# Layer-1 keys of a two-layer transformer: where tile 0's values and features stand in the order of work

## The chip, the cores and the metric

One core of a Trainium2 chip runs the whole network in one launch. Its engines work side by side, each through its own list of instructions in a fixed order: TensorE (PE) multiplies matrices, VectorE (DVE), ScalarE (ACT) and GpSimd (POOL) work on elements, SyncE (SP) issues transfers. They meet only at semaphores. The metric is the device time in microseconds; lower is better.

## The reference

The network has two layers of attention and experts over 2048 tokens of width 512, with a layer norm after each of the four blocks. The change is in the third block, layer 1's linear attention. Cut to what matters:

```python
x = _layernorm(x + _L0_ffn_ref(...))      # experts of layer 0: x + shared + routed
# _L1_attn_ref, 16 heads of width 32, 64 features
Q, K, V = heads(x @ qw + qb), heads(x @ kw + kb), heads(x @ vw + vb)
feature_map = lambda t: jax.nn.elu(t @ fw1 + fb1) @ fw2 + fb2
Qm, Km = feature_map(Q), feature_map(K)
KV = jnp.einsum('bhsf,bhsd->bhfd', Km, V)
Z = Km.sum(axis=2)
num = jnp.einsum('bhsf,bhfd->bhsd', Qm, KV)
den = jnp.einsum('bhsf,bhf->bhs', Qm, Z)[..., None]
out = (num / jnp.maximum(den, 1e-06)).transpose(0, 2, 1, 3).reshape(b, s, D) @ ow + ob
```

KV and Z are sums over all tokens, so every token's keys, values and features come first (the stage of keys), and the queries use them afterwards (the stage of queries).

## The kernel before

The tokens lie in 16 tiles of 128. Every fp32 product is made of three passes over two halves of each number (`_hi` and `_lo`, `mm3`, lines 66 to 68). The stage of keys is `attention1_keys`; all engines start it together after the experts of layer 0, and all start the queries together after it. In it the steps are, with i a tile and n a half of a pair of tiles (pair c holds tiles 2c and 2c+1; its halves are n = 2c and 2c+1):

- combine(i), "adding" in the title: GpSimd issues the gathers of the tile's two expert results (L1344; combine(i) issues those of tile i+1, once the buffer is free), VectorE adds them onto the residual (L1572, L1574) and takes the statistics of the layer norm (L93, L95).
- rstd(c), on GpSimd: one over the standard deviation of the pair's tiles (L100, L102).
- normalise(c), on VectorE: the pair's two tiles are normalised (L106).
- turn(n): TensorE transposes one half of the pair's columns into bank 0 (L1406), ScalarE copies out the high part (L1470), VectorE the low part (L1539). Bank 0 is one buffer, so turn(n) waits for the low part of turn(n-1).
- keys(n): 24 matmuls of 256 columns into bank 2 (k_kw), read by ScalarE (L1480) and VectorE (L1548).
- tile(i): 12 matmuls of 512 columns for the values (k_vw) and 16 of 256 for the features (a_fw, L1456) on TensorE. VectorE adds the bias to the values (L1560), ScalarE splits them (L1486) and applies Exp and Relu to the features (L1492, L1493), VectorE takes the low part and joins the two (L1563, L1567), and GpSimd adds the values to a running sum (L1383).
- before_tile(i) and after_tile(i), the end of a tile: ScalarE and GpSimd split the features (L1500, L1389), then TensorE adds the tile's products into KV: 16 small matmuls, L1430 and L1432, called sums(i) below.

The order is written out by hand in `schedule`, and each engine walks through the same list and does its own part of each step; an engine without a part in a step skips it. Up to pair 2 the list is written line by line, then a loop over the tiles runs 6 tiles ahead with combine, 4 halves ahead with turn, 2 ahead with keys. No planner changes this.

Of the kernel before, what the change touches and what calls it, by code (L numbers as in the profile page):

```python
# [31 lines left out]
NT = T // P  # L32
# [1202 lines left out]
def attention1_keys(k, xt, w):  # L1235
# [5 lines left out]
    with ExitStack() as ctx:  # L1241
# [42 lines left out]
        def schedule(turn=idle, keys=idle, tile=idle, before_tile=idle, after_tile=idle, combine=idle, rstd=idle, normalise=idle):  # L1284

            combine(0)
            combine(1)
            rstd(0)  # L1290
            normalise(0)
            combine(2)
            turn(0)
            turn(1)
            combine(3)
            rstd(1)
            keys(0)
            normalise(1)
            keys(1)
            turn(2)  # L1300
            turn(3)
            combine(4)
            combine(5)
            rstd(2)
            normalise(2)
            for i in range(NT):
                if i + 6 < NT:
                    combine(i + 6)
                    if i % 2:
                        rstd((i + 5) // 2)  # L1310
                if i + 4 < NT:
                    turn(i + 4)
                if i + 2 < NT:
                    keys(i + 2)
                if i % 2 and i + 6 < NT:
                    normalise((i + 5) // 2)
                if i:
                    before_tile(i - 1)
                tile(i)
                if i:  # L1320
                    after_tile(i - 1)
            before_tile(NT - 1)
            after_tile(NT - 1)

        with nc.Block() as block:
# [15 lines left out]
            def _(pool):  # L1341
# [43 lines left out]
                def tile_end(i):  # L1385
                    for n in (2 * i, 2 * i + 1):
# [3 lines left out]
                                           ALU.subtract).then_inc(s_glo, 1)  # L1390

                schedule(tile=tile, before_tile=tile_end, combine=combine, rstd=rstd)

            @block.tensor
            def _(pe):
# [40 lines left out]
                def tile(i):  # L1436
# [12 lines left out]
                    for n in (2 * i, 2 * i + 1):  # L1449
# [7 lines left out]
                        mm.then_inc(s_g, 1)  # L1457

                schedule(turn, keys, tile, after_tile=sums)

            @block.scalar
            def _(act):
# [32 lines left out]
                def tile_end(i):  # L1495
                    if i >= 2:
                        act.wait_ge(s_kv, i - 1)
                    for n in (2 * i, 2 * i + 1):
                        act.wait_ge(s_gf, n + 1)
                        act.activation(g_hi[:, i % 2, (n % 2) * CH:(n % 2 + 1) * CH], gf[:, n % 2, :], ACT.Copy).then_inc(s_ghi, 1)  # L1500

                schedule(turn, keys, tile, before_tile=tile_end)

            @block.vector
# [1204 lines left out]
```

## Time and profile before

| | us |
|---|---|
| median of 3 runs | 1599.05 |
| lowest and highest | 1598.6, 1601.68 |
| the profiled execution itself | 1595.75 |

The page's first part, busy time of each engine over the span (share, instructions), and two lines of its second, where each digit is the busy share or the TensorE clock in one fortieth of the span (some 40 us):

```profile
PE 1354.6 (85%) x7253; PEld 1117.2 (70%) x7253; DVE 1075.5 (67%) x1794; ACT 728.8 (46%) x1157; POOL 735.1 (46%) x654
...
PE   5999869999699999936999689996788899999960
...
PEclk8899979999799999968999789997798799999985
```

The stage of keys lies from 688 to 903 us of the span. A low digit of PE is a place where TensorE waits; the fraction of a microsecond is seen only in the timeline of each engine, where a row gives a start, a length, the instruction, and the idle time before it with the work that ended it.

### The profile page before, as it was taken

The numbers are of one execution on the slowest core, as the hardware profiler recorded it, in microseconds if no ns is written. First come the engines' busy times: TensorE is split into PE (matmuls) and PEld (weight loads), VectorE is DVE, ScalarE is ACT, GpSimd is POOL, SyncE is SP. The second block draws the span as 40 slices with busy tenths as digits, with TensorE's granted clock in tenths as the row PEclk, the third lists the DMA queues.
The fourth block names the chain that finished last, engine by engine and source line by source line (L and its number), as shares of the span: only waits on it lengthen the run. The fifth ranks groups of instructions, "written<-read, shape, count | busy, mean of one in ns | idle before, by whom it ended". The sixth has DMA issues, their size and how long they took to land. (4 is left out here: it accounts for less than half of the span.)

```text
span 1594.0 us, 21478 instructions
## 1 busy us (share of the span) xinstructions
PE 1354.6 (85%) x7253; PEld 1117.2 (70%) x7253; DVE 1075.5 (67%) x1794; ACT 728.8 (46%) x1157; POOL 735.1 (46%) x654
## 2 busy tenths in 40 slices
PE   5999869999699999936999689996788899999960
PEld 5787647766377777726999688985566777777740
DVE  5688757232388888865885556674493688888857
ACT  4121132000188888822555354440422488888850
POOL 1445510000488887634664233431055466666634
PEclk8899979999799999968999789997798799999985
DMA  4000040000456566642110000000513899999958
GB/s 166 1 1 27 27 133 2 1 0 0 173 189 215 174 214 220 226 119 55 53 41 1 34 1 1 27 27 27 195 40 115 317 340 344 346 348 344 344 132 316
DMA packets 81807, 212.67 MB, mean 133 GB/s; under 512 B 20425, under 2 KB 23497, under 8 KB 79291
## 3 DMA queue, kind: packets, MB, share of 16 engines
q1 hardware_dynamic: 50075, 133.14, 22.8%
q0 software_dynamic: 31120, 77.38, 17.2%
q8 instruction: 51, 0.84, 0.2%
q10 hardware_dynamic: 528, 1.05, 0.2%
q14 instruction: 33, 0.27, 0.1%
HBM read 208.75 MB, written 46.79 MB: 160 GB/s over the span
## 5 line engine op out<-in xcount | busy, mean ns | idle before, releaser
L66 PE MATMUL bank<-e_w_hi,e_xt_hi 128*96 128x384 f32 (+1 forms) x444 | 168.8, 380 | 3.4 <-DVE e_w_lo L2563 3.4
L2453 POOL DMA_INDIRECT sums<-e_y,r_target_of x64 | 121.8, 1902 | 88.4 <-DMA sums<-e_y,r_target_of 69.7
L68 PE MATMUL bank<-e_w_hi,e_xt_lo 128*96 128x384 f32 (+1 forms) x444 | 161.3, 363 | 0.0
L67 PE MATMUL bank<-e_w_lo,e_xt_hi 128*96 128x384 f32 (+1 forms) x444 | 160.8, 362 | 0.0
L1064 POOL DMA_INDIRECT e_w_raw<-in_w_gate_up,r_load_of x47 | 53.6, 1141 | 215.4 <-issue 215.4
L1189 DVE TENSOR_TENSOR e_w_lo<-e_w_raw,e_w_hi 128x2048 fp32r<-128x2048 f32 x47 | 107.8, 2293 | 33.7 <-ACT e_w_hi L1148 33.7
L2563 DVE TENSOR_TENSOR e_w_lo<-r_w_early,e_w_hi 128x1536 fp32r<-128x1536 f32 x48 | 84.4, 1758 | 24.3 <-ACT e_w_hi L2527 24.3
L1056 POOL DMA_INDIRECT e_xg<-rows,r_token_of x47 | 93.1, 1980 | 14.3 <-issue 14.3
L231 POOL TENSOR_TENSOR a_read<-a_read_n 128x256 f32<-128x256 f32 x64 | 50.3, 785 | 103.0 <-DVE a_read_n L452 103.0
L1687 POOL TENSOR_TENSOR q_g_lo<-q_gf,a_g 128x512 fp32r<-128x512 f32 x32 | 41.6, 1299 | 112.9 <-ACT a_g L1801 112.9
L1148 ACT ACTIVATE e_w_hi<-e_w_raw 128x2048 fp32r<-128x2048 f32 x47 | 89.7, 1909 | 0.0
L66 PE MATMUL bank<-e_w_hi,e_ht_hi 128*96 128x512 f32 (+1 forms) x222 | 87.6, 395 | 2.4 <-DVE e_ht_lo L2575 1.2
L67 PE MATMUL bank<-e_w_lo,e_ht_hi 128*96 128x512 f32 (+1 forms) x222 | 87.3, 393 | 0.0
L68 PE MATMUL bank<-e_w_hi,e_ht_lo 128*96 128x512 f32 (+1 forms) x222 | 87.1, 392 | 0.0
L66 PEld LDWEIGHTS bank<-e_w_hi,e_xt_hi 128*96 128x96 f32 (+1 forms) x444 | 77.4, 174 | 12.3 <-DVE e_w_lo L2563 3.6
L68 PEld LDWEIGHTS bank<-e_w_hi,e_xt_lo 128*96 128x96 f32 (+1 forms) x444 | 77.4, 174 | 11.7
L67 PEld LDWEIGHTS bank<-e_w_lo,e_xt_hi 128*96 128x96 f32 (+1 forms) x444 | 77.8, 175 | 8.6
L66 PE MATMUL bank<-s_xt_hi,s_w_hi 128*128 128x512 f32 (+1 forms) x192 | 76.9, 401 | 0.8 <-ACT s_scores L2212 0.8
L68 PE MATMUL bank<-s_xt_hi,s_w_lo 128*128 128x512 f32 (+1 forms) x192 | 76.1, 396 | 0.0
L67 PE MATMUL bank<-s_xt_lo,s_w_hi 128*128 128x512 f32 (+1 forms) x192 | 75.6, 394 | 0.0
L2527 ACT ACTIVATE e_w_hi<-r_w_early 128x1536 fp32r<-128x1536 f32 x48 | 71.2, 1484 | 0.0
L1072 POOL DMA_INDIRECT e_w_raw<-in_w_down,r_load_of x47 | 60.6, 1290 | 16.4 <-issue 16.4
(461 smaller groups left out, 4335.0 us busy)
## 6 DMA issues: line engine op xcount, KB each, us to landing
r_w_early<-in_w_gate_up SPq DMA_DIRECT2D x48, 768.0 KB, 16.0
r_w_early<-in_w_down SPq DMA_DIRECT2D x24, 768.0 KB, 12.9
results<-e_y SPq DMA_DIRECT2D x47, 256.0 KB, 3.7
rows<-resid SPq DMA_DIRECT2D x8, 1024.0 KB, 4.3
r_w_first<-in_w_gate_up SPq DMA_DIRECT2D x8, 768.0 KB, 15.9
e_w_raw<-in_w_down SPq DMA_DIRECT2D x8, 768.0 KB, 13.2
e_w_raw<-in_w_gate_up SPq DMA_DIRECT2D x8, 768.0 KB, 15.5
resid<-in_x SPq DMA_DIRECT2D x4, 1024.0 KB, 11.5
```

What stands on the lines that cost most here:

```text
L66: pe.matmul(out, a_hi, b_hi, start=start, stop=False)
L67: pe.matmul(out, a_hi, b_lo, start=False, stop=False)
L68: return pe.matmul(out, a_lo, b_hi, start=False, stop=stop)
L231: pool.tensor_tensor(read_2[:, v % 2, :], read_n[:, v % 2, 0:256], read_n[:, v % 2, 256:512], ALU.add).then_inc(s_r2, 1)
L1056: pool.indirect_dma_start(xg[p][:, :], None, k.rows, bass.IndirectOffsetOnAxis(k.token_of[:, c:c + 1], 0)).then_inc(s_g[p], 16)
L1064: pool.indirect_dma_start(w1_raw[p][:, :], None, io["w_gate_up0"], bass.IndirectOffsetOnAxis(k.load_of[:, c:c + 1], 0), bounds_check=E0 * ...
L1072: pool.indirect_dma_start(w2_raw[p][:, :], None, io["w_down0"], bass.IndirectOffsetOnAxis(k.load_of[:, c:c + 1], 0), bounds_check=E0 * P - ...
L1148: act.activation(w1_hi[p][:, :], w1_raw[p][:, :], ACT.Copy).then_inc(s_whi, 1)
L1189: vec.tensor_tensor(w1_lo[p][:, :], w1_raw[p][:, :], w1_hi[p][:, :], ALU.subtract).then_inc(s_wlo, 1)
L2453: pool.indirect_dma_start(k.sums[p % 2], bass.IndirectOffsetOnAxis(k.target_of[:, e:e + 1], 0), y[p][:, :], None, compute_op=ALU.add).then ...
L2527: act.activation(w1_hi[p][:, :, :], w1_raw[p][:, :, :], ACT.Copy).then_inc(s_whi, 1)
L2563: vec.tensor_tensor(w1_lo[p][:, :, :], w1_raw[p][:, :, :], w1_hi[p][:, :, :], ALU.subtract).then_inc(s_wlo, 1)
```

## The change

Tile 0's values and features come right behind turn(3) and combine(4), ahead of combine(5); keys(2) comes ahead of normalise(2) and of turn(4); combine(6) and turn(4) are written out, and the loop starts at tile 1 with the same steps as before. The same instructions run on each engine; only the order is another.

```diff
             turn(2)
             turn(3)
             combine(4)
+            tile(0)
             combine(5)
             rstd(2)
+            keys(2)
             normalise(2)
-            for i in range(NT):
+            combine(6)
+            turn(4)
+            for i in range(1, NT):
                 if i + 6 < NT:
                     combine(i + 6)
                     if i % 2:
...
-                if i:
-                    before_tile(i - 1)
+                before_tile(i - 1)
                 tile(i)
-                if i:
-                    after_tile(i - 1)
+                after_tile(i - 1)
```

On VectorE, from the end of combine(4) on, the order before reads as follows (resid is the residual, k_yg a gathered result, mv mean and variance, a_xt_lo the low part of a turn, k_k_lo that of the keys, k_vf the values):

```order
L1572 SCALAR_TENSOR_TENSOR resid<-k_yg,r_weight,resid 128x512
L1574 SCALAR_TENSOR_TENSOR resid<-k_yg,r_weight,resid 128x512
L93 BN_STATS stats<-resid 128x6
L95 BN_AGGR mv<-stats 128x2
L106 TENSOR_SCALAR resid<-resid,mv,rstd 128x512 x2
L1572 SCALAR_TENSOR_TENSOR resid<-k_yg,r_weight,resid 128x512
L1574 SCALAR_TENSOR_TENSOR resid<-k_yg,r_weight,resid 128x512
L93 BN_STATS stats<-resid 128x6
L95 BN_AGGR mv<-stats 128x2
L1539 TENSOR_TENSOR a_xt_lo<-bank,a_xt_hi 128x2x256
L1548 SCALAR_TENSOR_TENSOR k_k_lo<-bank,k_kb,k_k_hi 128x256 x2
L1560 TENSOR_TENSOR k_vf<-bank,k_vb 128x16x32
```

and in the changed kernel, whose lines stand two further down:

```order
L1562 TENSOR_TENSOR k_vf<-bank,k_vb 128x16x32
L1565 TENSOR_TENSOR k_v_hl<-k_vf,k_v_hl 128x8x66
L1569 SCALAR_TENSOR_TENSOR k_gf<-k_ex,k_gf 128x512 x2
L1574 SCALAR_TENSOR_TENSOR resid<-k_yg,r_weight,resid 128x512
L1576 SCALAR_TENSOR_TENSOR resid<-k_yg,r_weight,resid 128x512
L93 BN_STATS stats<-resid 128x6
L95 BN_AGGR mv<-stats 128x2
L1550 SCALAR_TENSOR_TENSOR k_k_lo<-bank,k_kb,k_k_hi 128x256 x2
L106 TENSOR_SCALAR resid<-resid,mv,rstd 128x512 x2
L1574 SCALAR_TENSOR_TENSOR resid<-k_yg,r_weight,resid 128x512
L1576 SCALAR_TENSOR_TENSOR resid<-k_yg,r_weight,resid 128x512
L93 BN_STATS stats<-resid 128x6
```

The three steps of tile 0 (k_vf, k_v_hl, k_gf) moved ahead of combine(5), and the low part of keys(2) ahead of normalise(2); the low part of turn(4) stays behind combine(6), and after it both orders are the same. TensorE's order changes alike: before turns 2, 3, 4, keys(2), tile(0), turn(5); now turns 2, 3, tile(0), keys(2), turns 4, 5.

On GpSimd, behind the zeroing in combine(4), before (a_vsum is the running sum of the values, a_g the features' low part):

```order
L1344 DMA k_yg<-results,r_slot 128x512 x2
L100 TENSOR_SCALAR var<-mv 128x2
L102 TENSOR_TENSOR rstd<-var,neg_half 128x2
L1344 DMA k_yg<-results,r_slot 128x512 x2
L1383 TENSOR_TENSOR a_vsum<-a_vsum,k_vf 128x528
L1344 DMA k_yg<-results,r_slot 128x512 x2
L100 TENSOR_SCALAR var<-mv 128x2
L102 TENSOR_TENSOR rstd<-var,neg_half 128x2
L1389 TENSOR_TENSOR a_g<-k_gf,a_g 128x512 x2
```

and now:

```order
L1385 TENSOR_TENSOR a_vsum<-a_vsum,k_vf 128x528
L1346 DMA k_yg<-results,r_slot 128x512 x2
L100 TENSOR_SCALAR var<-mv 128x2
L102 TENSOR_TENSOR rstd<-var,neg_half 128x2
L1346 DMA k_yg<-results,r_slot 128x512 x4
L100 TENSOR_SCALAR var<-mv 128x2
L102 TENSOR_TENSOR rstd<-var,neg_half 128x2
L1391 TENSOR_TENSOR a_g<-k_gf,a_g 128x512 x2
```

The sum of tile 0's values moved from behind the gathers of tile 7 to ahead of those of tile 6; the gathers of tiles 7 and 8 now follow each other behind the rstd of pair 2.

## Rows read from the trace of the kernel before

**Rows 1.** The page: the span of the profiled execution.

```profile
span 1594.0 us, 21478 instructions
```

**Rows 2.** Windows of the stage: us, busy (x) of each engine, clock, DMA.

```profile
792.00:802.00 10.00, 10.00 (x77) 9.48 (x76) 8.54 (x12) 4.91 (x10) 6.44 (x7) 1.00 0.16 48
```

**Rows 3.** Waits from 688 to 905 us: total, times, longest us.

```profile
PE bank L1406 <- DVE resid L106: 30.0, 2, 21.7
...
PE bank L1430 <- POOL a_g L1389: 5.0, 2, 3.1
```

**Rows 4.** TensorE timeline: start, length, instruction, [idle before <-releaser].

```profile
728.73 0.66 PE L1406 MATMUL bank<-ident,resid 128*128 128x128 f32 x4 [2.00 <-DVE a_xt_lo L1539]
737.73 1.12 PE L1406 MATMUL bank<-ident,resid 128*128 128x128 f32 x4 [8.34 <-DVE resid L106]
738.49 0.56 PE L66 MATMUL bank<-a_xt_hi,k_kw_hi 128*128 128x256 f32 x1
...
743.08 0.39 PE L66 MATMUL bank<-k_vw_hi,a_xt_hi 128*128 128x512 f32 x1
...
747.75 0.60 PE L1406 MATMUL bank<-ident,resid 128*128 128x128 f32 x4
748.10 0.36 PE L66 MATMUL bank<-a_xt_hi,k_kw_hi 128*128 128x256 f32 x1
...
751.03 0.39 PE L66 MATMUL bank<-k_vw_hi,a_xt_hi 128*128 128x512 f32 x1
...
757.78 0.33 PE L1430 MATMUL bank<-k_v_hl,a_g 128*128 128x132 f32 x1 [1.91 <-POOL a_g L1389]
...
759.90 1.11 PE L1406 MATMUL bank<-ident,resid 128*128 128x128 f32 x4
760.67 0.56 PE L66 MATMUL bank<-a_xt_hi,k_kw_hi 128*128 128x256 f32 x1
...
764.49 0.39 PE L66 MATMUL bank<-k_vw_hi,a_xt_hi 128*128 128x512 f32 x1
```

**Rows 5.** VectorE timeline of the same stretch.

```profile
733.05 0.72 DVE L1572 SCALAR_TENSOR_TENSOR resid<-k_yg,r_weight,resid 128x512 f32<-128x512 f32 x1
...
735.32 0.18 DVE L95 BATCH_NORM_AGGREGATE mv<-stats 128x2 f32<-128x6 f32 x1
736.67 1.00 DVE L106 TENSOR_SCALAR resid<-resid,mv,rstd 128x512 f32<-128x512 f32 x2 [1.16 <-POOL rstd L102]
737.59 0.74 DVE L1572 SCALAR_TENSOR_TENSOR resid<-k_yg,r_weight,resid 128x512 f32<-128x512 f32 x1
...
739.98 0.66 DVE L1539 TENSOR_TENSOR a_xt_lo<-bank,a_xt_hi 128x512 fp32r<-128x512 f32 x1
...
746.06 0.69 DVE L1560 TENSOR_TENSOR k_vf<-bank,k_vb 128x512 f32<-128x512 f32 x1 [1.03 <-PE bank L68]
...
751.45 0.75 DVE L1572 SCALAR_TENSOR_TENSOR resid<-k_yg,r_weight,resid 128x512 f32<-128x512 f32 x1
...
755.20 2.81 DVE L106 TENSOR_SCALAR resid<-resid,mv,rstd 128x512 f32<-128x512 f32 x2
```

**Rows 6.** ScalarE timeline of the same stretch.

```profile
747.44 1.28 ACT L1492 ACT_TABLE_LOAD   x1
...
751.96 1.15 ACT L1500 ACTIVATE a_g<-k_gf 128x512 fp32r<-128x512 f32 x2
```

**Rows 7.** GpSimd timeline of the same stretch.

```profile
736.83 1.33 POOL L1344 DMA_INDIRECT k_yg<-results,r_slot  x1 [0.20 <-issue]
738.46 1.48 POOL L1344 DMA_INDIRECT k_yg<-results,r_slot  x1 [0.30 <-issue]
746.83 1.32 POOL L1383 TENSOR_TENSOR a_vsum<-a_vsum,k_vf 128x528 f32<-128x528 f32 x1 [6.89 <-DVE k_vf L1560]
...
755.04 2.68 POOL L1389 TENSOR_TENSOR a_g<-k_gf,a_g 128x512 fp32r<-128x512 f32 x2
```

**Rows 8.** Landing of all gathers into the tiles k_yg.

```profile
DMA to landing us min/median/max: 3.3/3.6/7.9
```


## The prediction

> **What bounds the kernel now.** I read the windows first, since they tell which engine a saving has to reach. In the stage of keys TensorE is busy all of each of the twelve windows of 10 us from 762 to 882 us; one stands in [rows 2]: 10.00 of 10.00 at the full clock, VectorE 8.54. So from 762 us on TensorE sets the pace, and all engines leave the stage together. What TensorE has behind it when it comes to the first sums is therefore worth its full length at the end, unless VectorE, with 1.5 us of slack in 10, becomes the pacemaker.
>
> The waits come next. In [rows 3] TensorE waited 30.0 us in two waits for normalised tiles (21.7 is the start of the stage, which the change leaves alone; the other is 8.34) and 5.0 us in two for GpSimd's features (3.1 is the last tile; the other is 1.91). Then the timeline, where both gaps have a place: [rows 4] has the 8.34 us ahead of turn(4) at 737.73 and the 1.91 us ahead of sums(0) at 757.78. Behind each gap the granted clock fell to the lower of its levels (1.2 instead of 2.4 GHz): turn(4) with keys(2) took 743.08 - 737.73 = 5.35 us where turn(5) with keys(3) took 751.03 - 747.75 = 3.28, and turn(6) with keys(4) took 764.49 - 759.90 = 4.59.
>
> [Rows 5] show what the 8.34 us were: VectorE added tiles 4 and 5 and waited for rstd, while TensorE already had all that tile(0) needs. The change puts tile(0), 4.67 us of TensorE (743.08 to 747.75 in [rows 4]), and keys(2) there.
>
> **The change part by part.** Nothing is removed or added; every term is a move. Up to 733 us both orders are the same, so I follow the new order from there on the old scale.
>
> *tile(0) on TensorE* follows turn(3), which issues from 728.73 for some 0.4 us. It starts at about 729.1. Its values reach VectorE 2.98 us after their start (743.08 to 746.06, [rows 4, 5]), at 732.1; VectorE is busy with tile 4 until 733.1 [rows 5], which hides them, and would hide 1.0 us of a lower clock too. At the lower clock throughout, the values take at most twice as long, 735.1, and everything below moves by up to 2.0 us; the 0.66 us of turn(3) against 1.12 of turn(4) is the nearest row and shows the high clock at 728.73, so I take none. TensorE ends tile(0) at 733.8 and keys(2), 2.93 us at the high clock (748.10 to 751.03), at 736.7.
>
> *tile(0) on VectorE* costs 5.39 us from its first instruction to the next step (746.06 to 751.45), with ScalarE's table load of 1.28 us in it [rows 6]; the load is needed wherever tile(0) stands. So combine(5) starts at 733.1 + 5.4 = 738.5 instead of 733.05: the chain that turn(4) waits for gets 5.4 us later, and that is the price. It ends 2.45 later (733.05 to 735.50) at 740.95; rstd gives 1.17 (735.50 to 736.67), 742.1; the low part of keys(2), 0.88 us, now lies inside that wait and costs nothing. normalise(2) takes 0.92 to the next step, combine(6) 2.39 (737.59 to 739.98), the low part of turn(4) 0.66 and 0.15 to TensorE: 743.1, 745.4, 746.2. Turn(5) starts on TensorE at 746.2 where it started at 747.75: first term, 1.5 us gained.
>
> *turn(4)* itself starts 1.06 behind normalise(2)'s start, at 743.2, so TensorE idles 6.5 us from 736.7 and 2 us more ahead of turn(5). The 8.34 us aren't filled; 7.6 us of work go in and the wait grows by 5.4.
>
> *turn(5), keys(3), tile(1)* follow without a wait: keys(3) needs the halves of keys(2), done at 743. With keys(3) comes the second term. At the high clock turn and keys cost 3.28, with one cold stretch from the start 4.59 to 5.35. Turn(5) comes behind a broken gap, so part of it is cold; the clock's rise could fall anywhere in it. Bounds 749.5 and 751.6; I take 750.8, nearer to the cold row. tile(1) takes 4.7 more (the step of 4.67 above): 755.5.
>
> *sums(0)* needs the features' low part. ScalarE copies keys(3) and gives the first features 1.5 us behind keys(3)'s end (751.03, second row of [rows 6], the first of its two instructions, to 752.5), so at 752.3; GpSimd needs 2.68 [rows 7]: 755.0. Before, this work began only at 755.04, because rstd(3) stood ahead of it and waited for combine(7). combine(7) now starts at 747.5 (below) and rstd(3) is through at 751.1. So sums(0) starts at 755.5 against 757.78, 2.3 us: the 1.5 of turn(5), less 1.3 given up to the clock, and some 2 us of a gap that goes.
>
> *The clock behind sums(0)* is the third term. TensorE now runs on without a gap from 746.2, so I expect turn(6) and keys(4) at the high clock: 4.59 - 3.28 = 1.3 us. Bounds: 0 if the clock falls again, 1.3.
>
> *Gathers.* GpSimd has the sum of tile 0's values, 1.32 us, from 733.8 ahead of the gathers of tile 6. Their second is issued at 735.3 + 1.6 = 736.9 and lands 3.6 us later [rows 7, 8], 740.5, wanted at 743.1. Those of tile 7 stand behind rstd: issued second at 743.9, landed 747.5, wanted by combine(7) at 746.1. That wait of 1.4 us is new; it delays VectorE, but rstd(3) at 751.1 is still ahead of the 752.3 at which its successor could start. The gathers of tile 8 follow at 745.
>
> *VectorE behind it.* normalise(3) stands beside GpSimd's 2.68 us and took 2.81 [rows 5] against 1.00 for normalise(2), which stood beside gathers. Now both start near 752.5, and tile(1) follows at 755.4 instead of 757.93. In the next tile VectorE reaches the values within 0.5 us of TensorE's giving them, so the lead of TensorE holds, barely.
>
> The trace shows one of the two waiting for the other in that pair. By the Trainium skill (page "SBUF — State Buffer", section "Who interferes with whom") the pair is an exclusive lock and whoever starts first keeps it for the whole instruction. The trace agrees on the size, 2.81 beside 2.68. By that rule normalise(3), should it come first, would push GpSimd's work back by its own 1.0 us, sums(0) would start at 756.1, and the sum would be 3.0 us instead of 3.6.
>
> Sum: 2.3 + 1.3 = 3.6 us, 0.23%. Span 1594.0 [rows 1] to 1590.4, the profiled execution's 1595.75 to 1592.2. The median of the runs shown is 3.3 us above that execution, and the measured time will be such a median: 1599.05 - 3.6 = 1595.4. Low end of the terms: tile(0) late by 1.0 more than its cover, turn(5) and keys(3) at 5.35, the clock falling again: sums(0) at 757.3, a gain of 0.5. High end: keys(3) at 749.5, sums(0) at 754.2, a gain of 4.9.
>
> **The rivals.**
> 1. *The clock falls again.* For it: each of the two gaps before was followed by a cold stretch, and the new order has two again, 6.5 and 2 us. Against: the new gaps end before 746.2, well ahead of turn(6). If it is keys(3) that is cold throughout and keys(4) a part, the gain is 1.5 + 0.4 = 1.9, time 1597.2. The Trainium skill ("TensorE: Matmul & The Clock Gate", section "What's actually happening") calls the throttled clock the default which activity releases; by that, keys(3) is as cold as keys(2) was, and the sum would be some 0.8 us less than mine.
> 2. *VectorE becomes the pacemaker.* For it: it is 8.54 of 10 busy and reaches tile(1) only 2.5 us earlier, so no more than 2.5 can be kept: 1596.6. Against: it had waits for TensorE's values before, such as 1.03 us at 746.06.
> 3. *The move only exchanges waits.* If the waits before turn(4) and turn(5) grow by all that went in (rstd or the additions slower than their rows), turn(5) starts at 747.7, keys(3) is cold, and sums(0) starts at 757.5: 1598.8.
> 4. *Slower: the gathers of tile 7 land late.* They are now issued at 743.9, 5.4 us later than at 738.46 [rows 7], and wanted 5.3 us earlier. With landing L, sums(0) can't start before 743.9 + L + 2.39 + 1.17 + 2.68 = 750.1 + L. This decides from L = 5.4 and makes the kernel slower from 7.7. The longest of [rows 8] is 7.9, at the stage's start among other transfers; it gives 758.0 and, with a cold keys(4), 1599.3. Slower by over 0.2% needs 10.9, which no row shows.
>
> **How the numbers follow.** Chances: my forecast 0.6; rival 1 0.16; rival 2 0.1; rival 3 0.08; rival 4 0.06. Predicted time: 1595.4. A difference of 0.2%, 3.2 us, is about what a measurement of this kernel can tell from no change, and the forecast lies just beyond it. Within my case the gain is over 3.2 us in some three of four, 0.45, and a scatter of medians of 1 to 2 us carries a little over from the others: faster 0.48, same 0.46, slower 0.06. The range takes the high end with that scatter and the rivals to no change: 1592.8 to 1599.6.
>
> **What would show it.** TensorE's timeline: the values of tile 0 directly behind turn(3), at the high clock; a gap of 6 to 7 us ahead of turn(4) and about 2 ahead of turn(5); none ahead of sums(0); keys(4) in 2.9 us. VectorE: combine(5) some 5.4 us later than before, combine(7) behind a short wait for a gather. It is wrong if TensorE gets a new gap between sums(0) and the sums of tile 4, if turn(5) is not earlier than 747 on this scale, or if the windows behind 762 us fall below 10.00 for TensorE.

## The result and the profile after

The changed kernel takes 1595.58 us (median of 20 runs, 1592.98 to 1600.28) against 1599.05 (20 runs, 1597.2 to 1603.25). The ratio is 0.998, with a 95% interval of 0.997 to 0.9989: 3.5 us faster (1.8 to 4.8), where 3.6 was forecast.

The profiled execution is not a typical one, and that has to be read first. The span on the page:

```profile
span 1598.5 us, 21478 instructions
```

Its span is 4.5 us longer than that of [rows 1], and its own time, 1600.28, is the longest of the 20 runs. It is late before the changed part begins: turn(0) starts at 715.63 instead of 709.75, 5.9 us. So all times below are read against a point inside the stage, the start of turn(3) (728.73 in [rows 4]).

TensorE's timeline in this first profile of the change (start, length, instruction, [idle before <-releaser]):

```profile
734.84 1.06 PE L1408 MATMUL bank<-ident,resid 128*128 128x128 f32 x4 [2.00 <-DVE a_xt_lo L1541]
735.55 0.78 PE L66 MATMUL bank<-k_vw_hi,a_xt_hi 128*128 128x512 f32 x1
...
739.70 0.28 PE L66 MATMUL bank<-a_fw_hi,k_k_hi 128*128 128x256 f32 x1
...
749.99 1.11 PE L1408 MATMUL bank<-ident,resid 128*128 128x128 f32 x4 [5.41 <-DVE resid L106]
753.03 1.12 PE L1408 MATMUL bank<-ident,resid 128*128 128x128 f32 x4 [1.92 <-DVE a_xt_lo L1541]
...
758.97 0.39 PE L66 MATMUL bank<-k_vw_hi,a_xt_hi 128*128 128x512 f32 x1
...
763.64 0.22 PE L1432 MATMUL bank<-k_v_hl,a_g 128*128 128x132 f32 x1
...
765.34 0.66 PE L1408 MATMUL bank<-ident,resid 128*128 128x128 f32 x4
...
768.68 0.39 PE L66 MATMUL bank<-k_vw_hi,a_xt_hi 128*128 128x512 f32 x1
```

The reader is to see tile(0) (735.55) directly behind turn(3), the two gaps of 5.41 and 1.92 us ahead of turn(4) and turn(5), and no gap ahead of sums(0) at 763.64, where [rows 4] has 1.91. But the values take 739.70 - 735.55 = 4.15 us up to the features and reach VectorE 4.35 us behind their start (739.90 below), where [rows 4, 5] have 2.98, and turn(5) with keys(3) takes 758.97 - 753.03 = 5.94 us. turn(6) with keys(4) is at the high clock, 768.68 - 765.34 = 3.34, where [rows 4] has 4.59. sums(0) itself is faster too: 765.34 - 763.64 = 1.70 us, where [rows 4] has 759.90 - 757.78 = 2.12.

VectorE and GpSimd in the same execution:

```profile
739.90 0.69 DVE L1562 TENSOR_TENSOR k_vf<-bank,k_vb 128x512 f32<-128x512 f32 x1 [0.25 <-PE bank L68]
...
745.29 0.75 DVE L1574 SCALAR_TENSOR_TENSOR resid<-k_yg,r_weight,resid 128x512 f32<-128x512 f32 x1
...
754.41 0.75 DVE L1574 SCALAR_TENSOR_TENSOR resid<-k_yg,r_weight,resid 128x512 f32<-128x512 f32 x1 [1.44 <-DMA k_yg<-results,r_slot]
...
760.84 2.79 DVE L106 TENSOR_SCALAR resid<-resid,mv,rstd 128x512 f32<-128x512 f32 x2
```

```profile
750.73 0.95 POOL L1346 DMA_INDIRECT k_yg<-results,r_slot  x1 [0.30 <-issue]
...
760.61 2.73 POOL L1391 TENSOR_TENSOR a_g<-k_gf,a_g 128x512 fp32r<-128x512 f32 x2 [2.58 <-ACT a_g L1502]
```

From the values of tile 0 to combine(5) VectorE takes 745.29 - 739.90 = 5.39 us, as in [rows 5]. combine(7) waits 1.44 us for a gather. normalise(3) again takes 2.79 us beside GpSimd's 2.73.

TensorE's waits in the stage, and a window in its steady part:

```profile
PE bank L1408 <- DVE resid L106: 27.4, 2, 22.0
...
PE bank L1432 <- POOL a_g L1391: 3.1, 1, 3.1
```

```profile
798.00:808.00 10.00, 10.00 (x75) 9.42 (x74) 8.54 (x12) 5.20 (x11) 7.17 (x7) 1.00 0.13 36
```

The waits for normalised tiles fall from 30.0 us in [rows 3] to 27.4, those for GpSimd's features from 5.0 to the 3.1 of the last tile. The steady part is as in [rows 2]: in this window, as in the eleven others from 768 to 888 us, TensorE is busy 10.00 of 10.00 at the full clock.

### The profile page after: what moved, and what is told of

Same layout as the page of the kernel before. It is cut to its first block and busy times, and to the rows that moved or that the text cites. A ratio compares the mean times of both kernels' runs of the same rounds, so it can differ in the third digit from the quotient of the medians.

```text
span 1598.5 us, 21478 instructions
## 1 busy us (share of the span) xinstructions
PE 1358.8 (85%) x7253; PEld 1120.0 (70%) x7253; DVE 1076.8 (67%) x1794; ACT 730.2 (46%) x1157; POOL 745.2 (47%) x654
## 5 line engine op out<-in xcount | busy, mean ns | idle before, releaser
L2455 POOL DMA_INDIRECT sums<-e_y,r_target_of x64 | 110.4, 1726 | 76.6 <-DMA sums<-e_y,r_target_of 53.0
```

Of the source, the lines that this page charges most:

```text
L2455: pool.indirect_dma_start(k.sums[p % 2], bass.IndirectOffsetOnAxis(k.target_of[:, e:e + 1], 0), y[p][:, :], None, compute_op=ALU.add).then ...
```

## The experiments

Each is compared with the kernel before on its own chip, whose median was 1598.52 us for e1, e2, e4 and e5, 1598.19 for e3, e7, r1 and r2, 1597.76 for e8 and e9, and 1597.17 for e7b and e9b. "Stage" is the time from the start of turn(0) to SyncE's first transfer of the queries, in the profile of that run: 903.54 - 709.75 = 193.79 us before, 907.71 - 715.63 = 192.08 in the change's first profile. Ahead of turn(3), where no order was changed, the stage takes 18.5 to 19.8 us from one profile to the next, and the rest of the program varies too; so a stage is one execution's and not a median's.

| run | median, us | ratio (95% interval) | stage, us |
|---|---|---|---|
| the change | 1595.58 | 0.998 (0.997 to 0.9989) | 192.08 |
| e1, tile(0) alone | 1598.83 | 1.0005 (0.9994 to 1.0017) | 193.89 |
| e2, keys(2) alone | 1596.58 | 0.9988 (0.9975 to 1.0002) | 193.67 |
| e4, change kept warm | 1593.2 | 0.9963 (0.9951 to 0.9976) | 187.56 |
| e5, before kept warm | 1594.54 | 0.9976 (0.9967 to 0.9985) | 191.79 |
| e3, e2 with features first | 1591.7 | 0.996 (0.9948 to 0.9972) | 188.35 |
| e7, TensorE ahead | 1589.24 | 0.9942 (0.9929 to 0.9955) | 187.13 |
| e8, change, table early | 1592.66 | 0.9967 (0.9957 to 0.9977) | 189.96 |
| e9, e7, table early | 1591.97 | 0.9965 (0.9953 to 0.9978) | 185.77 |
| e7b, e7 again | 1589.42 | 0.9951 (0.9936 to 0.9965) | 185.05 |
| e9b, e9 again | 1592.27 | 0.9963 (0.9951 to 0.9976) | 187.78 |
| r1, the change again | 1594.72 (one run) | | 189.83 |
| r2, before again | 1598.45 (one run) | | 193.74 |

**Both kernels once more (r1, r2).** No edit.

> The change once more, one look, for its profile. Theory A (where TensorE's clock falls and rises shifts from one execution to the next, and the first profile had tile(0) and keys(3) cold): turn(5) with keys(3) anywhere between 3.3 and 5.9 us, the stage between 188 and 193 us from turn(0) to the start of the queries. Rival (the first profile shows the change's fixed course): 192.1 us again, keys(3) in 5.2, and the gain of 3.5 us of the medians lies outside the stage.

> The kernel before once more, one look, for its profile. Theory A: turn(4) with keys(2) between 3.3 and 6.1 us, and the stage between 192 and 195 from turn(0) to the start of the queries; so that single pairs of profiles differ by 0 to 6 us where the medians differ by 3.5. Rival: 193.8 again.

TensorE in the second profile of the change:

```profile
730.51 0.66 PE L1408 MATMUL bank<-ident,resid 128*128 128x128 f32 x4 [2.00 <-DVE a_xt_lo L1541]
...
730.92 0.48 PE L66 MATMUL bank<-k_vw_hi,a_xt_hi 128*128 128x512 f32 x1
...
733.79 0.28 PE L66 MATMUL bank<-a_fw_hi,k_k_hi 128*128 128x256 f32 x1
...
744.94 1.12 PE L1408 MATMUL bank<-ident,resid 128*128 128x128 f32 x4 [6.27 <-DVE resid L106]
747.91 1.11 PE L1408 MATMUL bank<-ident,resid 128*128 128x128 f32 x4 [1.85 <-DVE a_xt_lo L1541]
...
752.58 0.39 PE L66 MATMUL bank<-k_vw_hi,a_xt_hi 128*128 128x512 f32 x1
...
757.25 0.22 PE L1432 MATMUL bank<-k_v_hl,a_g 128*128 128x132 f32 x1
...
758.95 0.66 PE L1408 MATMUL bank<-ident,resid 128*128 128x128 f32 x4
...
762.28 0.39 PE L66 MATMUL bank<-k_vw_hi,a_xt_hi 128*128 128x512 f32 x1
```

This is the course that was forecast. The values run at the high clock (2.87 us to the features), turn(5) starts 17.40 us behind turn(3) (17.5 forecast, 19.02 in [rows 4]), sums(0) 26.74 behind it (26.8 forecast, 29.05 before), and turn(6) with keys(4) takes 3.33. VectorE still waited 0.34 us for the values of tile 2, in both profiles of the change. The stage is 3.9 us shorter than before, in the first profile 1.7. The kernel before repeated itself to 0.05 us. The difference between the two profiles of the change is in where TensorE's clock falls and rises: 4.15 against 2.87 us for the values of tile 0, 5.94 against 4.67 for turn(5) with keys(3). Theory A holds for the change; its wider spread for before isn't shown by two profiles.

**One part at a time (e1, e2).** The edits, against the changed kernel:

```diff
 e1:  rstd(2)                     e2:  combine(4)
-     keys(2)                    -     tile(0)
      normalise(2)                     combine(5)
      combine(6)                       rstd(2)
      turn(4)                          keys(2)
+     keys(2)                          normalise(2)
                                       combine(6)
                                       turn(4)
                                 +     tile(0)
```

> Only tile(0) moves ahead of combine(5); keys(2) stays behind turn(4). On the scale of the profile before: turn(4) starts at 743.2 as in the change, but turn(4) and keys(2) then cost TensorE a cold 5.35 us, so turn(5) starts at 748.5 (before 747.75, the change 746.2 by its forecast). Theory A (both moves are needed, tile(0) fills the gap at a price of 5.4 us on VectorE and keys(2) makes up for it): sums(0) near 756.5, keys(4) at the high clock, 1 to 2.6 us under before, 1596.5 to 1598, and slower than the change by 1 or more. Rival B (tile(0) alone is the gain, keys(2) is neutral): the same as the change, 1595.6.

> Only keys(2) moves ahead of normalise(2) and turn(4); tile(0) stays behind turn(4). Its VectorE part lies in the wait for rstd, so turn(4) still starts at 737.7, tile(0) follows it and turn(5) comes at 743 to 744.5, 3 us before its old place. sums(0) then waits for GpSimd, whose rstd(3) stands behind combine(7): 754.8. Theory A: a gain of 3 us without the price on VectorE, 1596.0, about as fast as the change; turn(5) well ahead of where the change has it, and a gap of 2 us ahead of sums(0) with the clock falling behind it. Rival B (the gain comes from tile(0) in the gap): 1598 or more.

TensorE in e1, then in e2:

```profile
750.07 1.11 PE L1408 MATMUL bank<-ident,resid 128*128 128x128 f32 x4 [8.25 <-DVE resid L106]
...
757.95 0.36 PE L66 MATMUL bank<-a_xt_hi,k_kw_hi 128*128 128x256 f32 x1 [1.50 <-DVE k_k_lo L1550]
```

```profile
738.51 1.03 PE L1408 MATMUL bank<-ident,resid 128*128 128x128 f32 x4 [2.75 <-DVE resid L106]
...
745.25 0.60 PE L1408 MATMUL bank<-ident,resid 128*128 128x128 f32 x4
...
755.29 0.33 PE L1432 MATMUL bank<-k_v_hl,a_g 128*128 128x132 f32 x1 [1.92 <-POOL a_g L1391]
...
758.37 1.11 PE L1408 MATMUL bank<-ident,resid 128*128 128x128 f32 x4
```

Tile(0) alone is worth nothing: TensorE's gap ahead of turn(4) is 8.25 us as before, because tile(0) moved turn(4) away by 6.4 us (34.34 us behind turn(0), 27.98 before): its 5.4 us on VectorE, and most of the rest because turn(3) and the values ran cold. keys(3) also waits for the low part of the keys just made, 1.50 us that I had not counted. So sums(0) comes 30.64 us behind turn(3) (765.55 - 734.91), 1.6 later than before, and its high clock and that of turn(6) and keys(4) give 1.7 back; Theory A's gain of 1 to 2.6 us didn't come. That is the rival "the move only exchanges waits", and it is what the change would be without keys(2). Rival B is excluded: the intervals of e1 and of the change don't meet. In e2 turn(4) comes after a gap of 2.75 and turn(5) 17.04 us behind turn(3) (745.25 - 728.21), earlier than in the change, but 1.2 us or more later than expected. keys(2) ran cold there, VectorE waited 1.38 us for it with normalise(2) behind it, and turn(4) starts 10.30 us behind turn(3) instead of 9.00; then the values ran cold. The gap of 1.92 ahead of sums(0) stays, and the clock falls behind it: sums(0) takes 3.08 us (758.37 - 755.29). 1.9 us faster than before, with an interval that touches no change, is less than the 3 of theory A. The intervals of e2 and of the change overlap, so the times don't show how much tile(0) adds to keys(2).

**The clock by itself (e4, e5).** Matmuls whose result nobody reads fill TensorE's gaps.

```diff
                 def turn(n):
                     c, half = n // 2, n % 2
+                    for f in range({4: 22, 5: 7}.get(n, 0)):        # e5: {4: 34}, and 7 in sums(0)
+                        pe.matmul(bank[7][:, :], xt_hi[:, f % KD, 0:P], kw_hi[:, f % KD, :], start=True, stop=True,
+                                  skip_group_check=True)
```

> The change, with 22 extra matmuls of 512 columns on TensorE ahead of turn(4) and 7 ahead of turn(5), into a bank that nobody reads yet; they are 5.0 and 1.6 us of work in gaps of 5.4 and 1.9. Theory A (the clock behind the gaps is a term): turn(5) and keys(3) in 3.3 us instead of 5.9, a gain over the change of up to 1.3 us at sums(0), where GpSimd's features become the bound: 1593.5 to 1594.5, and less scatter between runs. Rival C (VectorE and GpSimd hide the cold stretch): 1595.6, as the change, though the matmuls are fast.

> The kernel before, with 34 extra matmuls of 512 columns ahead of turn(4) (7.8 us in a gap of 8.34) and 7 ahead of sums(0) (1.6 in 1.91). It moves no work, so it prices the clock alone. Theory A: turn(4) with keys(2) in 3.3 instead of 5.35, keys(4) with turn(6) in 3.3 instead of 4.6: 2.1 + 1.3 = 3.4 us, 1595.7, as much as the change without moving anything. Rival C (hidden): within 1 us of before, 1598 to 1599.

TensorE in e4, then in e5:

```profile
748.89 0.66 PE L1410 MATMUL bank<-ident,resid 128*128 128x128 f32 x4 [0.75 <-DVE a_xt_lo L1543]
...
752.24 0.39 PE L66 MATMUL bank<-k_vw_hi,a_xt_hi 128*128 128x512 f32 x1
...
756.90 0.22 PE L1434 MATMUL bank<-k_v_hl,a_g 128*128 128x132 f32 x1
```

```profile
744.39 0.60 PE L1408 MATMUL bank<-ident,resid 128*128 128x128 f32 x4
...
747.68 0.39 PE L66 MATMUL bank<-k_vw_hi,a_xt_hi 128*128 128x512 f32 x1
...
752.36 0.60 PE L1408 MATMUL bank<-ident,resid 128*128 128x128 f32 x4
...
762.42 0.33 PE L1434 MATMUL bank<-k_v_hl,a_g 128*128 128x132 f32 x1 [0.30 <-POOL a_g L1389]
```

In e4 turn(5) with keys(3) takes 3.35 us instead of 5.94 or 4.67, and sums(0) follows tile(1) without a gap. The time is 5.3 us under before, beyond the change's 3.5 (the two intervals still overlap a little), and GpSimd didn't become the bound. In e5 turn(4) with keys(2) takes 3.29 instead of 5.35, although the 34 matmuls ran past the gap and turn(4) starts 9.95 us behind turn(3) (734.44 in that profile) instead of 9.00. This kernel moves no work and is still 4.0 us faster than before (interval 2.4 to 5.3). So rival C is out. The gaps of the kernel before cost, by the medians, as much through the clock behind them as the whole change gives.

**The gap ahead of sums(0) (e3).** e2, and the loop's first pass written out with the end of tile 0 ahead of rstd(3):

```diff
+            combine(7)
+            turn(5)
+            before_tile(0)
+            rstd(3)
+            keys(3)
+            normalise(3)
+            tile(1)
+            after_tile(0)
-            for i in range(1, NT):
+            for i in range(2, NT):
```

> keys(2) alone moved (as in the run e2), and beyond it the first pass of the loop written out with before_tile(0) directly behind combine(7) and turn(5), so that GpSimd's low part of tile 0's features no longer stands behind rstd(3). Theory A (TensorE's starts and gaps up to sums(0) set the end, and the clock behind them): the gap of 1.92 us ahead of sums(0) goes and with it the cold turn(6) and keys(4); 2 + 1.3 us under e2: 1593.3. Rival D (VectorE is the pacemaker once TensorE leads by 3 us more): TensorE gets new gaps at turn(6) or at the values of tile 2, and the time stays at e2's 1596.6.

TensorE in e3:

```profile
758.08 0.22 PE L1440 MATMUL bank<-k_v_hl,a_g 128*128 128x132 f32 x1
...
759.78 0.66 PE L1416 MATMUL bank<-ident,resid 128*128 128x128 f32 x4
...
763.12 0.39 PE L66 MATMUL bank<-k_vw_hi,a_xt_hi 128*128 128x512 f32 x1
```

The gap is gone, turn(6) with keys(4) takes 3.34 us, and 4.5 us came off e2 (6.5 under before against 1.9), where 3.3 was expected of a gap of 1.92 and a clock. The price of the clock was put too low: in e2 sums(0), turn(6) and keys(4) took 763.59 - 755.29 = 8.30 us, in e3 763.12 - 758.08 = 5.04, so it cost 3.3 there and not 1.3. Rival D, the waiting at e2's time, is excluded.

**TensorE ahead of the others (e7, e9).** e7 is e3 with TensorE's part of tile(0) moved by itself; the other engines keep theirs behind turn(4):

```diff
             keys(2)
+            early(0)
             normalise(2)
...
-                schedule(turn, keys, tile, after_tile=sums)
+                schedule(turn, keys, lambda i: i and tile(i), after_tile=sums, early=tile)
```

> As e3, and TensorE alone does tile(0) directly behind keys(2), ahead of turn(4); ScalarE, VectorE and GpSimd keep their part of tile(0) behind turn(4). It fills TensorE's gap as the change does, without the 5.4 us that the change puts on VectorE ahead of combine(5). Theory A: turn(4) 9.0 us behind turn(3) as before, turn(5) 3 us behind turn(4), sums(0) 6 us or more ahead of its place before: 1592 to 1593. Rival D (VectorE the pacemaker): TensorE waits again at turn(6) or at the next values, and the time is that of e3 or of the change kept warm, 1593 to 1594.

> The order of the run e7 again, beside e9's on one chip, since their times came from two chips. Theory A (the order is what counts, and the early table load is worth at most the 0.7 us gap ahead of sums(0)): 8 to 9 us under before. Rival (the first time was a lucky one): 6 to 7 us under before, as e3.

TensorE in e7b:

```profile
741.95 0.27 PE L1417 MATMUL bank<-ident,resid 128*128 128x128 f32 x1
...
743.96 0.66 PE L1417 MATMUL bank<-ident,resid 128*128 128x128 f32 x4 [1.41 <-DVE a_xt_lo L1550]
...
752.85 0.33 PE L1441 MATMUL bank<-k_v_hl,a_g 128*128 128x132 f32 x1 [0.72 <-POOL a_g L1400]
...
754.93 0.66 PE L1417 MATMUL bank<-ident,resid 128*128 128x128 f32 x4
```

turn(4) follows tile(0) without a gap, turn(5) comes 13.24 us behind turn(3) (730.72 in that profile) instead of 19.02, and the wait ahead of sums(0) is 0.72. The order was 9.0 us under before in e7 and 7.8 in e7b, faster than both kernels. That is some 3 us more than e7's Theory A had. In its two profiles the stage is 6.7 and 8.7 us shorter than before, and what lies behind the stage is shorter as well, 689.0 and 689.2 us against 690.5 and 691.2. By the median it is the fastest order of all; but e3 alone has 6.5 of it, and the intervals of e3 and e7 overlap, so what TensorE's part of tile(0) adds to e3 isn't settled. e7b's interval leaves its rival, 6 to 7 us, open too.

e8 and e9 add one Exp of a single column at ScalarE's start of the stage, to the change and to e7:

```diff
                 act.wait_ge(s_kb, 16)
+                act.activation(pre[:, :], kb[:, 0:1], ACT.Exp)
```

> The change, with one Exp of a single column at ScalarE's start of the stage, so that the table load of 1.28 us no longer lies in tile(0). Theory A (every microsecond of tile(0) on VectorE delays combine(5), rstd, normalise(2), combine(6) and with them turn(5)): tile(0) takes 4.3 instead of 5.4 us on VectorE, turn(4) and turn(5) start 1.1 us earlier, 1594.4 against the change's 1595.5. Rival (turn(5) is not set by that chain, or what it gains is lost ahead of sums(0)): 1595.5, as the change.

> The run e7 with the same early Exp. There tile(0) on VectorE stands ahead of combine(7), the features' low part and the low part of turn(5), and TensorE waited 0.71 us for GpSimd ahead of sums(0). Theory A: that gap of 0.7 us goes and nothing else, since the 1.41 us ahead of turn(5) is VectorE's combine(6): 1588.5. Rival D (VectorE sets the pace of the whole stage by then): 1.1 us or more, 1588.1 or less.

> The order of the run e9 again, on the same chip as e7. Theory A: within 1 us of e7's time. Rival D (VectorE's normalise(3) now comes too late for turn(6), where e9's profile has a gap of 1.21 us with a cold keys(4) behind it, and this costs more than the load gives back): 1 to 3 us slower than e7.

VectorE in e8:

```profile
739.71 0.69 DVE L1564 TENSOR_TENSOR k_vf<-bank,k_vb 128x512 f32<-128x512 f32 x1 [0.19 <-PE bank L68]
...
743.67 0.75 DVE L1576 SCALAR_TENSOR_TENSOR resid<-k_yg,r_weight,resid 128x512 f32<-128x512 f32 x1
```

tile(0) now takes 743.67 - 739.71 = 3.96 us instead of 5.39, turn(5) starts 16.68 behind turn(3) instead of 18.19 in the change's first profile, whose values were as cold as here. That is 1.5 us at turn(5) where 1.1 was expected, and 2.1 by the two ratios, whose intervals overlap. The chain holds; what lies beyond 1.5 is open.

On top of e7 the same edit made things worse, by 3.2 us in e9 (each against before on its chip) and by 2.9 in e9b, on one chip with e7b, though the intervals overlap; both expectations of e9 missed that, and the second of e9b has the size. VectorE and GpSimd in e7b:

```profile
749.99 1.68 DVE L1585 SCALAR_TENSOR_TENSOR resid<-k_yg,r_weight,resid 128x512 f32<-128x512 f32 x1
```

```profile
749.64 3.15 POOL L1400 TENSOR_TENSOR a_g<-k_gf,a_g 128x512 fp32r<-128x512 f32 x2 [1.08 <-ACT a_g L1511]
```

VectorE, GpSimd and TensorE in e9b:

```profile
748.86 0.75 DVE L1585 SCALAR_TENSOR_TENSOR resid<-k_yg,r_weight,resid 128x512 f32<-128x512 f32 x1
749.64 3.26 DVE L1587 SCALAR_TENSOR_TENSOR resid<-k_yg,r_weight,resid 128x512 f32<-128x512 f32 x1
```

```profile
749.79 2.56 POOL L1401 TENSOR_TENSOR a_g<-k_gf,a_g 128x512 fp32r<-128x512 f32 x2
```

```profile
756.18 0.66 PE L1418 MATMUL bank<-ident,resid 128*128 128x128 f32 x4 [1.21 <-DVE resid L106]
```

Without the table load VectorE starts combine(7) at 748.86. Its second addition starts at 749.64, 0.15 us ahead of GpSimd's two subtractions (749.79), and takes 3.26 us, where the first addition needs 0.75. It ends at 752.9, 0.6 us behind the second subtraction. rstd(3) and normalise(3) follow late, and turn(6) waits 1.21 us. In e7b the same two met as well, but there the addition started 0.35 us behind GpSimd and took 1.68, and the subtractions took 3.15 instead of 2.56: the addition ran between the two.

That explains the new wait, but not the longer time. e9's profile has the same addition of 3.26 us and the same wait of 1.21, with turn(6) and keys(4) in 4.85 us behind it, and still it needs no longer than e7 from turn(3) to the end of the stage, 167.3 us against 167.4. e9b, where turn(6) and keys(4) took 3.33, needs 168.1 against e7b's 166.5. What lies behind the stage takes 691.2 and 692.1 us in e9 and e9b, 2 to 3 us more than in e7 and e7b, though no order was changed there. Why the edit costs time on top of e7 stays open.

## Why the prediction was right

*Turn(5) 1.5 us earlier.* Right: 1.6 in the second profile, 0.8 in the first. There turn(3) itself ran cold (1.06 us, where the prediction took the 0.66 of [rows 4] as a reason to count no lower clock), which made VectorE 0.4 us late, and the cold values arrived another 0.25 us after it was free, so that the cover of 1.0 us that had been reckoned was used up.

*The price on VectorE, 5.4 us, and the gap of 6.5 that stays.* 5.39; gaps of 5.41 and 6.27, the shorter where tile(0) had run colder. e1 shows the price by itself.

*keys(3) at 750.8, 4.6 us with turn(5).* 4.67 and 5.94. The range given for this term ended at 5.35, the nearest row; the first profile went beyond it. The bound was too narrow. The size is a matter of the execution: the change has two gaps at which the clock may fall, and 22 and 7 matmuls that nobody reads took another 1.8 us off by the medians. Keys(3) as cold as keys(2), 5.35 us, the last variant of rival 1, lies between the two profiles; neither shows it.

*sums(0) 2.3 us earlier and without a gap.* 2.3 and 0.25.

*turn(6) and keys(4) at the high clock, 1.3 us.* 4.59 - 3.34 = 1.25 and 4.59 - 3.33 = 1.26. The sum left out sums(0) itself, part of which also ran at the lower clock before: 2.12 us against 1.70 in both profiles of the change, another 0.4. With it the second profile's 3.9 us are accounted for: 2.3 + 1.26 + 0.4. Rival 1 (the clock falls again) didn't occur behind sums(0); its other half, a fully cold keys(3), did in the first profile (753.80 to 758.97 on TensorE). That execution was the longest of its 20, but its stage is only 2.3 us longer than the second profile's; 4.2 us of the 5.6 between the two executions lie ahead of the stage.

*The gathers.* combine(7) waited 1.44 and 1.80 us, 1.4 forecast. Rival 4 stayed away: nothing after it moved.

*VectorE as pacemaker (rival 2).* Not at a lead of 2.3 us, nor at that of e3 and e4, since both went on gaining. A gap at turn(6) appears only in e9 and e9b. In e9b sums(0) comes 22.2 us behind turn(3), in e7b 22.1 without such a gap; so it isn't the lead that makes it, but the addition of 3.26 us.

*The rule on the shared port pair.* Its less favourable reading would have had normalise(3) come first and sums(0) 0.6 late. GpSimd was first by 0.2 us (760.61 against 760.84), and normalise(3) waited, as before. In the Trainium skill ("SBUF — State Buffer", section "Who interferes with whom") a VectorE instruction with two SBUF inputs contends with a GpSimd instruction that reads SBUF, and the issue order decides who blocks. The additions of e7b and e9b have two inputs in SBUF and agree with the first half: 1.68 and 3.26 us instead of 0.75. On the second half the recorded starts don't agree: in e9b the addition is recorded 0.15 us ahead of GpSimd and waited for both subtractions, in e7b 0.35 behind and waited for one.

*The size of the sum.* 3.6 forecast, 3.5 between the medians, and 1.7 and 3.9 in the two profiles of the stage. The two profiles bracket the forecast, and it left out the 0.4 us of sums(0); the agreement to 0.1 us is luck within a scatter of 7 us between single runs.

## What to carry to other kernels

When work is pulled forward into one engine's gap, each other engine's part of that work comes along and may push the gap away by as much. Here tile(0) alone gained nothing. An order that leaves tile(0) in place, moves keys(2) and puts tile 0's end ahead of rstd(3) gained 6.5 us, and with TensorE's part of tile(0) moved by itself 9.0 and 7.8, against the change's 3.5. And a gap on TensorE has a second price behind it: price a gap with the clock of what follows, and look at more than one profile before a term of a microsecond or two is called right.

## What the runs showed of the hardware

The place at which TensorE's granted clock changes isn't fixed in the program. In two profiles of the same kernel the same 12 matmuls behind turn(3) took 4.15 and 2.87 us, and turn(5) with keys(3) 5.94 and 4.67, with the same gaps ahead to within 1 us. In e9 and e9b turn(6) and keys(4) took 4.85 and 3.33 us behind the same gap of 1.21. Filling the gaps with matmuls that nobody reads was worth 4.0 us in the kernel before.

A VectorE addition with two SBUF inputs took 3.26 us instead of 0.75 beside two GpSimd subtractions of 2.56 us in all, when its recorded start was 0.15 us ahead of theirs (e9b). When it was 0.35 us behind (e7b), it took 1.68 and the subtractions 3.15. The five profiles with this meeting are all one or the other: e3 and e7 are like e7b, e9 is like e9b.
